# The last step of three layer norms, on ScalarE instead of VectorE

## The reference

```
def _layernorm(x, axis=-1, eps=1e-05):
    m = jnp.mean(x, axis=axis, keepdims=True)
    v = jnp.var(x, axis=axis, keepdims=True)
    return (x - m) / jnp.sqrt(v + eps)

x = _layernorm(x + attention(x))             # delta rule, convolutions, gated mixture of four sources
x = _layernorm(x + cross_attention(x, ctx))  # rotated queries and keys, decay mask, no softmax
x = _layernorm(x + experts(x))               # 8 experts of 128 -> 256 -> 128, the best two per token
```

## Time and profile before

| | before |
|---|---|
| median of 3 runs | 513.43 us |
| span of the profiled execution | 510.6 us |
| what lies around the span, against the median | 2.8 us |
| PE busy in the span | 401.5 us (79%) |
| DVE busy | 323.2 us (63%) |
| ACT busy | 159.2 us (31%) |
| chain that ended last, by engine | PE 49%, DVE 31%, issue 9%, DMA 5%, ACT 3% |
| mean granted TensorE clock | 0.843 |

### The profile page before, as it was taken

The page is one execution under the profiler, slowest core; times in us unless marked ns, Lnnn a source line. Parts: engine busy times, 40 slices in busy tenths (PEclk is TensorE's granted clock), DMA queues, the critical chain, the costliest instruction groups (busy, mean ns, idle before and its releaser), DMA issues.

```text
span 510.6 us, 8321 instructions
## 1 busy us (share of the span) xinstructions
PE 401.5 (79%) x2952; PEld 293.4 (57%) x2952; DVE 323.2 (63%) x1050; ACT 159.2 (31%) x267; POOL 39.3 (8%) x77
## 2 busy tenths in 40 slices
PE   1979999788973699984245689897998979887992
PEld 0647677467962699971023355565656546564672
DVE  2043464677999823368763576676897588777635
ACT  1252523512345211142021124422433244413430
POOL 7000000002980000000000000000000000000000
PEclk9989999997997555575555969999899989999997
DMA  7460201039653900000000000000020000000000
GB/s 246 105 186 1 42 0 22 1 75 296 166 145 88 119 3 3 3 2 0 1 1 27 15 21 1 0 22 0 2 62 2 21 0 21 0 0 1 22 2 21
DMA packets 48305, 22.23 MB, mean 44 GB/s; under 512 B 17768, under 2 KB 47632, under 8 KB 48016
## 3 DMA queue, kind: packets, MB, share of 16 engines
q1 hardware_dynamic: 31760, 13.40, 10.9%
q10 hardware_dynamic: 16512, 8.39, 6.0%
HBM read 18.64 MB, written 3.15 MB: 43 GB/s over the span
## 4 chain that ended last, share of the span: by engine, by line
PE 49%; DVE 31%; issue 9%; DMA 5%; ACT 3%; SPq 2%; DVEq 0%; ACTq 0%; POOL 0%
PE bank L460 9%; PE bank L493 5%; PE bank L691 5%; PE bank L699 5%; PE bank L721 5%; PE bank L733 4%; PE bank L442 4%; DVE prod L1430 3%; DVE inv L1432 3%; DVE as_t L1410 2%; DVE as_t L1232 2%; DVE nt L1143 2%; DVE nt L1142 2%; DVE as_t L1223 2%; DVE sm L1144 2%
## 5 line engine op out<-in xcount | busy, mean ns | idle before, releaser
L699 PEld LDWEIGHTS bank<-w_sb,as_t 128*128 128x128 f32 x512 | 61.0, 194 | 23.0 <-issue 18.8
L699 PE MATMUL bank<-w_sb,as_t 128*128 128x128 f32 x512 | 63.9, 280 | 5.0 <-ACT as_t L1002 5.0
L1002 ACT ACTIVATE as_t<-bank,cb 128x512 f32<-128x512 f32 x64 | 43.4, 687 | 76.0 <-PE bank L691 60.8
L691 PE MATMUL bank<-as_t,w_sb 128*128 128x512 f32 x128 | 66.5, 648 | 0.0
L1410 DVE SCALAR_TENSOR_TENSOR as_t<-bank,as_t 128x128 f32<-128x128 f32 x128 | 36.0, 344 | 23.4 <-PE bank L699 21.1
L460 PE MATMUL bank<-wtap,xc_pad 128*128 128x384 f32 x128 | 47.0, 514 | 3.8 <-DVE wtap L1157 3.8
L721 PE MATMUL bank<-vb,early 32*32 32x32 f32 x512 | 29.9, 236 | 11.7 <-DMA early<-inverses 11.7
L442 PE MATMUL bank<-ident,as_t 128*128 128x128 f32 (+1 forms) x64 | 12.1, 319 | 33.8 <-DVE as_t L1232 15.7
L1201 DVE TENSOR_TENSOR as_t<-bank,masks 128x512 f32 (+1 forms) x32 | 21.3, 690 | 26.7 <-PE bank L493 26.7
L460 PEld LDWEIGHTS bank<-wtap,xc_pad 128*128 128x128 f32 x128 | 25.0, 202 | 20.3 <-issue 4.3
L721 PEld LDWEIGHTS bank<-vb,early 32*32 32x32 f32 x512 | 28.2, 151 | 13.1 <-issue 12.3
(11 more groups left out here) (221 smaller groups left out, 647.5 us busy)
## 6 DMA issues: line engine op xcount, KB each, us to landing
toep<-taps_long ACTq DMA_DIRECT2D x8, 1024.0 KB, 7.0
toep<-x SPq DMA_DIRECT2D x8, 256.0 KB, 2.8
early<-x SPq DMA_DIRECT2D x4, 256.0 KB, 4.6
w_sb<-w SPq DMA_DIRECT2D x1, 1024.0 KB
w_sb<-w SPq DMA_DIRECT2D x2, 512.0 KB
blocks<-as_t SPq DMA_DIRECT2D x16, 64.0 KB, 2.0
early<-blocks SPq DMA_DIRECT2D x1, 1024.0 KB, 4.9
toep<-ctx_in SPq DMA_DIRECT2D x4, 256.0 KB, 3.4
```

Of the source, the lines that this page charges most:

```text
L691: pe.matmul(ps[4 + half][:, :], w1_sb[:, e, half * 128:half * 128 + 128], x2_c.rearrange("p b t -> p (b t)"), start=True, stop=True).then_ ...
L699: last = pe.matmul(bank(6 + e % 2)[:, b, :], hid[:, e % 2, half, b * L:(b + 1) * L], w2_sb[:, e, half, :], start=(half == 0), stop=(half = ...
L1002: act.activation(hid[:, e % 2, half, :], ps[4 + half][:, :], ACT.Relu, bias=c_of("b1", 2 * e + half)).then_inc(s["hid_ready"], 1)
```

## The change

The twelve times four TENSOR_SCALARs go. VectorE now ends a layer norm with one operation on 128 x 4 numbers that makes the shift (minus mean times inverse root), and signals `moments1`, `moments2` or `moments3`. ScalarE waits for that signal and does four Identity activations of 128 x 128, with the inverse root as scale and the shift as bias, each a number per partition read from memory. These ScalarE steps have a place in ScalarE's order: `x1_scaled(p)` ahead of `x1_columns(p)`, `x2_scaled(p)` ahead of `x2_columns(p)`, `result_scaled(q)` in the loop between `square_mixture(g)` and `ctx_columns(g)`, in the tail between `route_exp(p)` and `hidden(p, 0)`, and once more at the very end. `x1_ready`, `x2_ready` and `fin_ready` are now signalled by ScalarE. TensorE's order is the same.

```diff
--- before.py
+++ after.py
@@ -186,6 +186,8 @@
         y_g = over3(G, D)
         bn6 = over3(G, 6)
         mv = over3(G, 2)
+        ln_scale = over3(3, G)
+        ln_shift = over3(3, G)
         x1 = over3(G, D)
         x1_c = over3(G, L)
         qr = over3(G, L)
...
@@ -250,9 +252,9 @@
         CREDITS = {
             "pe": {"proj_ready": 1, "q_ps": 1, "kh_ps": 1, "kb_ps": 1, "gram_ps": 1,
                    "z_ps": 1, "st_ps": 1, "st2_ps": 1, "y_ps": 2},
-            "act": {"kb_c": 2, "proj_free": 2, "onc_ready": 1, "hid_ready": 2},
-            "dve": {"vb_ready": 1, "gram_kept": H, "x1_ready": 1, "x2_ready": 1, "ostats_ready": 1, "y_added": 2,
-                    "fin_ready": 1, "sum_started": 1},
+            "act": {"kb_c": 2, "proj_free": 2, "onc_ready": 1, "hid_ready": 2, "x1_ready": 1, "x2_ready": 1,
+                    "fin_ready": 1},
+            "dve": {"vb_ready": 1, "gram_kept": H, "ostats_ready": 1, "y_added": 2, "sum_started": 1},
             "pool": {"v_kept": 1},
         }
         credit = {n: k for of in CREDITS.values() for n, k in of.items()}
@@ -970,6 +972,27 @@
                 act.wait_ge(s["ont_ps"], g + 1)
                 act.activation(on_c, bank(0), ACT.Copy).then_inc(s["onc_ready"], 1)
 
+            def normalise(y, dst, which):
+
+                for b in range(G):
+                    last = act.activation(dst[:, b, :], y[:, b, :], ACT.Identity, bias=ln_shift[:, which, b:b + 1],
+                                          scale=ln_scale[:, which, b:b + 1])
+                return last
+
+            def x1_scaled(g):
+                act.wait_ge(s["moments1"], g + 1)
+                normalise(y_g, x1, 0).then_inc(s["x1_ready"], 1)
+
+            def x2_scaled(g):
+                act.wait_ge(s["moments2"], g + 1)
+                act.wait_ge(s["sum_started"], g + credit["sum_started"])
+                normalise(y_g, x2, 1).then_inc(s["x2_ready"], 1)
+
+            def result_scaled(g):
+                act.wait_ge(s["moments3"], g + 1)
+                act.wait_ge(stored, 16 * (g + 1))
+                normalise(acc, fin, 2).then_inc(s["fin_ready"], 1)
+
             def ctx_columns(g):
                 act.wait_ge(s["ct_ps"], g + 1)
                 act.activation(c_c, bank(2), ACT.Copy).then_inc(s["cc_ready"], 1)
@@ -1079,6 +1102,7 @@
 
 
                 p, q = g - 1, g - 2
+                x1_scaled(p)
                 x1_columns(p)
                 x_columns(g)
                 st_columns(g)
@@ -1086,10 +1110,13 @@
                 if experts_left:
                     hidden(q, 7)
                 source_exp(g)
+                x2_scaled(p)
                 x2_columns(p)
                 route_exp(p)
                 hidden(p, 0)
                 square_mixture(g)
+                if experts_left:
+                    result_scaled(q)
                 ctx_columns(g)
                 hidden(p, 1)
                 hidden(p, 2)
@@ -1121,6 +1151,7 @@
             hidden(p, 5)
             hidden(p, 6)
             hidden(p, 7)
+            result_scaled(p)
 
 
         @block.vector
@@ -1218,7 +1249,7 @@
                 mask_products(NG - 1, r)
 
 
-            def layernorm(y, dst, done):
+            def layernorm(y, which):
                 for b in range(G):
                     last = dve.bn_stats(out=bn6[:, b, :], in_=y[:, b, :])
                 own(last)
@@ -1227,11 +1258,10 @@
                     last = dve.bn_aggr(out=mv[:, b, :], in_=bn6[:, b, :])
                 own(last)
                 own(dve.tensor_scalar(sm1[:, 0:G], mv[:, :, 1], EPS, None, ALU.add))
-                rsqrt(sm2[:, 0:G], sm1[:, 0:G], G)
-                for b in range(G):
-                    last = dve.tensor_scalar(dst[:, b, :], y[:, b, :], mv[:, b, 0:1], sm2[:, b:b + 1],
-                                             ALU.subtract, ALU.mult)
-                last.then_inc(s[done], 1)
+                rsqrt(ln_scale[:, which, :], sm1[:, 0:G], G)
+                dve.scalar_tensor_tensor(out=ln_shift[:, which, :], in0=mv[:, :, 0], scalar=-1.0,
+                                         in1=ln_scale[:, which, :], op0=ALU.mult, op1=ALU.mult
+                                         ).then_inc(s[("moments1", "moments2", "moments3")[which]], 1)
 
             def head_sums(xs, squares, to, n):
 
@@ -1347,8 +1377,9 @@
             def x1_norm(g):
                 dve.wait_ge(s["wo_ps"], g + 1)
                 dve.wait_ge(xa_in, 16 * (g + 1))
+                dve.wait_ge(s["x2_ready"], g - 1 + credit["x2_ready"])
                 own(dve.tensor_tensor(out=y_g, in0=bank(1), in1=xa, op=ALU.add))
-                layernorm(y_g, x1, "x1_ready")
+                layernorm(y_g, 0)
 
             def rotate_keys(g):
                 dve.wait_ge(s["k_rot_ps"], g + 1)
@@ -1371,7 +1402,7 @@
                 dve.wait_ge(s["att_ps"], g + 1)
                 dve.wait_ge(s["x1_ready"], g + 1 + credit["x1_ready"])
                 own(dve.tensor_tensor(out=y_g, in0=bank(2), in1=x1, op=ALU.add))
-                layernorm(y_g, x2, "x2_ready")
+                layernorm(y_g, 1)
 
             def route_max(g):
                 dve.wait_ge(s["route_ps"], g + 1)
@@ -1414,8 +1445,7 @@
                 dve.wait_ge(s["y_added"], g * E + e + 1 + credit["y_added"])
 
             def finish(g):
-                dve.wait_ge(stored, 16 * (g + 1))
-                layernorm(acc, fin, "fin_ready")
+                layernorm(acc, 2)
 
             source_sums(3, 0, B, 1)
             dve.sem_inc(s["sums_ready"], 1)
```

More of the change, by code:

```diff
@@ L244, in decoder_kernel @@
                  "x2t_ps x2c_ready route_ps rmax_ready rexp_ready score_ready scoret_ps scoret_ready binit_ps hid_ps "
-                 "hid_ready y_ps sum_started y_added fin_ready").split()
+                 "hid_ready y_ps sum_started y_added fin_ready moments1 moments2 moments3").split()
         s = {n: sem(n) for n in names}
```

## The result

The changed kernel takes 549.4 us (median of 4 runs, 547.7 to 554.1) beside 513.4 before: 1.0715 times as long, interval 1.0667 to 1.0763. It is slower, as forecast, by 36 us in place of 30. Times that are given for whole runs are medians. The profiled execution took 547.7 us with a span of 545.9.

The account below looks back on a forecast made before the run. The ending chain was taken to run along VectorE in the loop, TensorE in the tail. Terms 1.26 + 14.1 + 8.6 + 0.64 + 5.75 = 30.35 us on a 510.6 span, plus 2.8 to the median, gave 543.8; range 529 to 550.

Parts of the forecast that it names:

- The other edits: First group's x1 and x2 cost 1.26 us, the last layer norm 0.64; moved waits and ScalarE's other new steps cost nothing.
- TensorE's clock: Lower clock behind three new TensorE stalls: 2.2 us for each loop step, 1.35 in the tail, 5.75 together, possibly zero.
- Price of Identity: The new ScalarE activation of 128 x 128: 0.46 us for one, 1.54 for four in a row.
- s: How much later each x1 and x2 comes in the first and second layer norm: 0.63 us, bounds -0.09 and +0.93.
- First group: First group's x1 and x2, on a chain with nothing beside them: 1.26 us later.
- Two loop steps: Loop steps 2 and 3: ScalarE waits at the third norm, delaying TensorE's `values` 7.05 us each, 14.1 together.
- Tail: Last group: the third norm's wait stands ahead of the first Relu, so TensorE's expert 1 comes 8.6 us later.
- End: Last layer norm, which ends the kernel: 0.64 us longer.
- The rivals: ScalarE's queue stall costs nothing, 516.2 us, chance 0.05; VectorE's relief decides, 509.7, 0.04; or Identity needs its own table load.
- The faster case: Second rival: VectorE's relief decides, given a free queue stall and four activations under 0.91 us; 509.7 us, chance 0.04.

Follow-up runs that it names:

- e5: Changed kernel plus nine one-element fills at the start of VectorE's program, moving its loop from instruction 528 to 537; 543.1 us, ratio 1.0621.
- e2: Changed kernel with the first two layer norms back on VectorE, only the third ending on ScalarE at the same places; 543.5 us, ratio 1.0593.
- e8: Changed kernel with x1, x2 and the last group's third norm back on VectorE, the other third norms later in ScalarE's order; 511.9 us, ratio 0.9969.
- e6: Changed kernel with the third norm later in ScalarE's order (last group's stays) and nine one-element fills starting VectorE's program; 522.7 us, ratio 1.0209.
- e7: e6 plus two matmuls on TensorE, results overwritten, ahead of its wait for x2; 514.3 us, ratio 1.0002.
- e10: Kernel before the change plus two matmuls on TensorE, results overwritten, ahead of its wait for x2; 518.7 us, ratio 1.0122.

## Why the prediction was wrong

The direction, the mechanism and the place were right, and the time was 5.6 us short: 543.8 forecast, 549.4 measured; by the ratio it is 550.1 (1.0715 x 513.4), just past the upper end of the range, 550.

**The step that failed** is "The other edits". It prices what the edits do to the order of work, and puts nothing for VectorE's program, which has nine instructions fewer ahead of its loop. This brought on a fetch at the loop's jump: 5.0 us between x1 and x2 of step 3 (23.0 beside e5's 18.0), and 6.3 us between the medians of the changed kernel and e5. Without it, in e5, the kernel takes 543.1 beside the 543.8 forecast. That the rest comes out so near is partly luck, since "TensorE's clock" was too small and the loop steps too large. By the prediction's own steps:

- **Price of Identity**, 0.46 and 1.54 for four: 0.48 and 1.65 measured, close. **s**, 0.63: between output and x1 transposes the changed kernel takes 0.73 to 0.84 longer, so s was 0.1 to 0.2 too small.
- **First group**, 1.26: 0.48 measured at the next output transposes (327.86 to 328.64, of which 0.30 was there ahead). The forecast was too much. What fits is that the lower level behind the first x2 ends near 303 us in both kernels (mean 0.58 and 0.55 from 300 to 303, 1.00 from 303 to 306), so that the later work had less of it.
- **Two loop steps**, 14.1, and clock 4.4: in the kernel with nothing else (e2) 9.1 a step, against 9.25 forecast. In the changed kernel only 6.4 and 7.6 were paid between x2 and the next output transposes, where the sum has 9.25 each. In step 2 TensorE, at the lower clock, was late for `values` by itself and waited 3.60 us there, beside 6.30 in e2; what step 3 saved isn't traced.
- **Tail**, 8.6: expert 1 comes 31.2 us late (471.86 to 503.06), 9.2 more than the last group's x1 transposes (22.05), where the 8.6 without its 0.63 for x1 is 8.0. The start of expert 1 before was read 0.2 too late (472.06). **End**, 0.64: 0.7 measured, right.
- **TensorE's clock**, 5.75: mis-sized. In the tail it had 1.35; from expert 1 to the last expert matmul 3.3 were lost. In the loop it counted only the stalls behind `moments3`. That the small growth of x2's wait and a stall of VectorE would hold the clock down too wasn't in the sum, though the earlier trace rows showed 3.4 us behind a shorter wait of the same place. From 303 us to the end of TensorE's work the lower level holds for some 43 us in the changed kernel (mean 0.91 up to 538) and some 13 in the kernel before (mean 0.97 up to 503). These 30 us more cost 15 at most, by an estimate from the two levels, and less where TensorE doesn't set the time.

In sum, up to the last group's x1 transposes: the loop was forecast 1.26 + 14.1 + 4.4 + 0.63 = 20.4 longer and is 21.7 longer, the tail 10.0 and is 13.2. The loop came near by luck: the 14.0 us that its two steps paid in place of 18.5 stood against a stall that wasn't forecast. The rivals fell as forecast: `values` waits, and no table load was added (15 before and after). The faster case needed a free queue and four activations in under 0.91 us; they take 1.65. Of the queue alone e8 is the test, and it gains 1.6 us.

One chain of runs prices the parts one after the other, by ratios to the kernel before: 1.0715 as changed, 1.0621 without the stall (5 us), 1.0209 with the third norm later (21 us), 1.0002 with the clock kept (11 us). The order matters: the last step removes all low clock behind x2, of which the kernel before has some too, and the steps can't be read as prices that add up in another order.

## What to carry to other kernels

Before an operation goes to a less busy engine, ask when its input is ready and what stands behind it in that engine's order: here a step that waited in a queue kept TensorE standing for 6.3 us and cost 9.1 us each time (e2), and the same work some steps later cost nothing (e8). On an engine whose program has a loop, count the instructions ahead of it before and after an edit; when the trace shows "issue" at the jump and more instruction packets, shift the loop or write it out. A stall on TensorE has to be priced with the lower clock that may follow it, and only where TensorE sets the time.

## What the runs showed of the hardware that was not expected

- VectorE's jump back costs 4.8 to 5.6 us of "issue" and five or six more packets of instructions in q14 with the loop at 528 or 656 (counted without waits and signals), and nothing with it at 537. Two packets of 8 KB run while it stands.
- In step 3 TensorE's idle time ahead of x2 grew from 1.2 to 1.9 us, and the stretch at the lower level behind it from 3.4 us (414 to 419, mean 0.66) to some 7 (417 to 426 in e6, means 0.58, 0.50, 0.79). Two matmuls in the idle time kept it at 1.00 (e7).
- A wait of 1.46 us left the clock at full, and one of 1.48 us at the same instruction a step later was followed by 15 us with means from 0.50 to 0.63 (e10).
